# Two mixture-of-experts layers rewritten: one unrolled run of slots for all sequences, gate weights spread by one product, weights split two experts at a time

## The chip, the cores and the metric

The kernel runs on one core of one Trainium2 chip. The time is the device time of one launch in microseconds (us), the median of three runs. Engines are TensorE (PE; PEld is its weight load), VectorE (DVE), ScalarE (ACT), GpSimd (POOL) and SyncE (SP), which here only issues DMAs. Each engine runs its own instructions in order and waits on semaphores.

## What is computed

Ten layers in a row on eight sequences of 512 tokens with 128 features: rwkv, attn0, moe0, alibi, attn0, moe0, light, moe1, diff, moe1. The change touches only the four expert layers. Both kinds normalise the tokens, score eight experts, pick two and add the weighted sum of their outputs:

```
moe0: logits = xf @ Wr.T + expert_bias;  rw = softmax(logits);  topw, topi = top_k(rw, 2);  topw = softmax(topw)
      combine = sum(one_hot(topi, 8) * topw, axis=1)
      out = swiglu(xf, shared) + sum_e combine[:, e] * (silu(xf @ eW1[e]) * (xf @ eW3[e])) @ eW2[e]
moe1: the same without the bias and the shared expert, hidden size 256 (two tiles of 128) instead of 128
```

All experts are computed for all tokens; the weight of an expert that was not chosen is 0.

## The kernel before

**Slots.** A slot is one expert on one sequence. moe0 has 9 slots to a sequence (the shared expert first, then eight), with one tile (HT = 1); moe1 has 8 slots with two tiles (HT = 2). Every product of float32 data is three matmuls on rounded halves (`product`, lines 373 to 375): high by high, low by high, high by low. For each tile of a slot, TensorE makes `h1` and `h3` (3 matmuls each of 512 columns), ScalarE makes `s = silu(h1)` (L3267), `sc = s * bcs` scales it by the gate weight (POOL, L3301, or DVE, L3358), VectorE makes `g = sc * h3` (L3366), ScalarE rounds it to `g_hi` (L3239), VectorE makes `g_lo = g - g_hi` (L3337), and TensorE adds the `down` product (3 matmuls) into one PSUM bank, LAG = 2 slots later. `h1` and `h3` have two PSUM banks each.

**Gate weights.** `broadcast_c` makes the weight of expert e, one number a token, into a tile with the same row in all 128 partitions: four fp32 transposes (L3168) of a column of `comb` that is read as if it were 128 columns, then a ScalarE copy to `bcs` (L3251). The scaling is on DVE for all moe0 slots, and in moe1 on DVE for slot 1 and on POOL for the other seven.

**Head.** During the slots of sequence j, `Head` prepares sequence j+1: statistics (DVE, L203, L207), scale (POOL, L217 to L231), normalised tokens `z` (four DVE instructions, L256 or L258), four transposes, `hi` (ACT), `lo` (DVE), the gate product (12 matmuls of 8 columns), and on DVE `gate_logits`, `gate_choice`, `gate_weights`. moe0 also needs four small powers on POOL (`gate_exp`, L3109); both need one (`gate_e2`, L3114). The constants `E_STATS` to `E_WEIGHTS` say in which slot a part stands.

**Loop.** The slots stand in a hardware loop (`Fori`) over four pairs of sequences. A pass holds the slots of two sequences and ends by draining: the last two `down`, the output copy `out`, four transposes `tail` and the addition to `x`. The waits in the loop compare with registers that are worked out by extra instructions.

**Weights.** `Weights` loads the matrix in pieces of 1024 columns and splits each into high (ACT) and low (DVE) halves. All pieces are split before the loop; TensorE waits for all of them, and the gate choice of sequence 0 stands behind them on DVE.

Of the kernel before, what the change touches and what calls it, by code (L numbers as in the profile page):

```python
# [2962 lines left out]
def moe_block(core, name, moe, weights_in, kind, src, add_to, bias, store=False):  # L2963

# [10 lines left out]
    with ExitStack() as ctx:
        sb = lambda n, s, t=F32: ctx.enter_context(nc.sbuf_tensor(name + n, s, t))
        head = Head(core, ctx, name, kind, src, TR)
        vec, act = Steps(nc, ctx, plan, name + "_vector"), Steps(nc, ctx, plan, name + "_scalar")
# [46 lines left out]
        def gate_tensor(t, k, par):
            h = head
            t.wait_ge(h.act.sem, h.act.done(k, "hi"))
            t.wait_ge(h.low.sem, h.low.done(k, "lo"))
            t.wait_ge(h.vec.sem, h.vec.done(k, "logits", back=1))
            for q in range(NQ):  # L3030
                c = slice(q * P, (q + 1) * P)
                ins = product3(nc, ps[:, GATE, q * 8:q * 8 + 8], h.hi[:, par, c], h.lo[:, par, c], w_hi[:, 0:8], w_lo[:, 0:8])
            ins.then_inc(h.pe.sem, h.pe.step("gate"))


        def gate_logits(d, k):

            h, v, n = head, head.vec, nc.vector
            inc = lambda ins, *key: ins.then_inc(v.sem, v.step(*key))
            wait = lambda *key: d.wait_ge(v.sem, v.done(k, *key))  # L3040
            gate = ps[:, GATE, 0:NQ * 8].rearrange("p (q e) -> p q e", e=8)
            d.wait_ge(h.pe.sem, h.pe.done(k, "gate"))
            if bias is None:
                inc(n.tensor_copy(logits[:, :, :], gate), "logits")
            else:
                inc(n.tensor_tensor(logits[:, :, :], gate, bias_sb[:, :].unsqueeze(1).to_broadcast([P, NQ, 8]), ALU.add), "logits")
                wait("logits")
                inc(n.tensor_reduce(lmax[:, :], logits[:, :, :], AXX, ALU.max), "lmax")
                wait("lmax")
                inc(n.tensor_tensor(hot1[:, :, :], logits[:, :, :], wide(lmax[:, :]), ALU.subtract), "shifted")  # L3050
                wait("shifted")
                inc(n.tensor_scalar(hot2[:, :, :], hot1[:, :, :], LOG2E, None, ALU.mult), "shifted2")  # L3052

        def gate_choice(d, k):

            h, v, n = head, head.vec, nc.vector
            inc = lambda ins, *key: ins.then_inc(v.sem, v.step(*key))
            wait = lambda *key: d.wait_ge(v.sem, v.done(k, *key))
            if bias is None:
                wait("logits")  # L3060
            else:
                d.wait_ge(h.pool.sem, h.pool.done(k, "ex", NQ - 1))
                inc(n.reduce_sum(lsum[:, :], ex[:, :, :], AXX), "lsum")
                wait("lsum")
                inc(n.reciprocal(den[:, :], lsum[:, :]), "lrec")
                wait("lrec")
                inc(n.tensor_tensor(logits[:, :, :], ex[:, :, :], wide(den[:, :]), ALU.mult), "rw")
                wait("rw")
            settle(core, d)
            for q in range(NQ):  # L3070
                inc(n.max(top[:, q, :], logits[:, q, :]), "top", q)
            wait("top", NQ - 1)
            settle(core, d)
            inc(n.tensor_tensor(diff[:, :], top[:, :, 1], top[:, :, 0], ALU.subtract), "diff")
            for q in range(NQ):
                inc(n.max_index(idx[:, q, :], top[:, q, :], logits[:, q, :]), "idx", q)
            wait("diff")
            inc(n.tensor_scalar(p1[:, :], diff[:, :], LOG2E, None, ALU.mult), "diff2")
            wait("idx", NQ - 1)
            inc(n.tensor_copy(idxf[:, :, :], idx[:, :, 0:2]), "idxf")  # L3080
            wait("idxf")
            it = core.iota[:, :].unsqueeze(1).to_broadcast([P, NQ, 8])
            inc(n.tensor_tensor(hot1[:, :, :], idxf[:, :, 0:1].to_broadcast([P, NQ, 8]), it, ALU.is_equal), "hot1")
            inc(n.tensor_tensor(hot2[:, :, :], idxf[:, :, 1:2].to_broadcast([P, NQ, 8]), it, ALU.is_equal), "hot2")

        def gate_weights(d, k, par):

            h, v, n = head, head.vec, nc.vector
            inc = lambda ins, *key: ins.then_inc(v.sem, v.step(*key))
            wait = lambda *key: d.wait_ge(v.sem, v.done(k, *key))  # L3090
            d.wait_ge(h.pool.sem, h.pool.done(k, "e2"))
            inc(n.tensor_scalar(den[:, :], e2[:, :], 1.0, None, ALU.add), "den")
            wait("den")
            inc(n.reciprocal(p1[:, :], den[:, :]), "p1")
            wait("p1")
            inc(n.tensor_tensor(p2[:, :], p1[:, :], e2[:, :], ALU.mult), "p2")
            inc(n.tensor_tensor(hot1[:, :, :], hot1[:, :, :], wide(p1[:, :]), ALU.mult), "c1")
            wait("p2")
            inc(n.tensor_tensor(hot2[:, :, :], hot2[:, :, :], wide(p2[:, :]), ALU.mult), "c2")
            wait("c2")  # L3100
            inc(n.tensor_tensor(comb[:, par, :, :], hot1[:, :, :], hot2[:, :, :], ALU.add), "comb")

        def wide(a):
            return a.unsqueeze(2).to_broadcast([P, NQ, 8])

        def gate_exp(p, k, q):
            h, o = head, head.pool
            p.wait_ge(h.vec.sem, h.vec.done(k, "shifted2"))
            nc.gpsimd.tensor_tensor(ex[:, q, :], core.two[:, 0:8], hot2[:, q, :], ALU.pow).then_inc(o.sem, o.step("ex", q))  # L3109

        def gate_e2(p, k):
            h, o = head, head.pool
            p.wait_ge(h.vec.sem, h.vec.done(k, "diff2"))
            nc.gpsimd.tensor_tensor(e2[:, :], core.two[:, 0:NQ], p1[:, :], ALU.pow).then_inc(o.sem, o.step("e2"))  # L3114
# [4 lines left out]

        @block.sync
        def _(sp):
            if bias is not None:
                sp.dma_start(bias_sb[:, :], bias.unsqueeze(0).to_broadcast([P, 8])).then_inc(bias_loaded, 16)
            weights_in.sync_part(sp)
            if store:

# [1 line left out]
                with sp.Fori(0, PAIRS) as i:  # L3130
# [379 lines left out]
```

## Time and profile before

| what | value |
|---|---|
| median of three runs | 3336.51 us (3334.9 to 3336.55) |
| profiled execution | 3339.98 us, its span 3338.2 us |
| granted TensorE clock over the span | 0.909 of full |
| busy, share of span | PE 82%, DVE 65%, POOL 47%, ACT 44% |
| first moe0 layer | 532.7 to 821.2 us |
| second moe0 layer | 1158.5 to 1446.9 us |
| first moe1 layer | 1990.8 to 2379.5 us |
| second moe1 layer | 2950.5 to 3338.2 us |

Busy time is the time in which an engine works, a wait is the idle time ahead of an instruction with the one that released it. The layers follow each other with a barrier, so a layer's length adds directly to the whole. The four expert layers are 1353 us of 3338. Matmuls are pipelined, so that the distance from the start of one to the start of the next says what one costs, not its duration.

### The profile page before, as it was taken

What the parts mean: (1) busy time and instruction counts of PE and PEld (TensorE: products, weight loads), DVE (VectorE), ACT (ScalarE), POOL (GpSimd) and SP (SyncE); (2) the same over time, 40 slices, a digit from 0 to 9 for tenths busy, and PEclk for the clock granted to TensorE, in tenths of its full rate; (3) what the DMA queues carried; (4) which work ended last, traced back from release to release, by engine and by line L of the source; (5) the groups of instructions that cost most, each with busy time, mean ns of one, the idle gap of its engine ahead of it and who ended that gap; (6) DMA issues with size and microseconds to landing.
All of it is one profiled execution on the core that took longest, in us unless ns stands there. A gap on an engine that the chain in (4) does not pass through costs nothing. (4 is left out here: it accounts for less than half of the span.)

```text
span 3338.2 us, 51906 instructions
## 1 busy us (share of the span) xinstructions
PE 2741.1 (82%) x14536; PEld 1879.4 (56%) x14536; DVE 2169.6 (65%) x5031; ACT 1460.2 (44%) x2255; POOL 1576.9 (47%) x1513
## 2 busy tenths in 40 slices
PE   3367897887769878869889878899799999978898
PEld 2245565665656556645545446667555555556666
DVE  5745764776567477756555556666577777766666
ACT  3433454544425444521111114555366666645554
POOL 5544754333136433344444434444666666634444
PEclk7678798998779989979999999999799999989999
DMA  1000210000011100010000010000000000010000
GB/s 31 0 12 2 48 31 22 0 0 15 0 33 40 32 1 0 1 49 1 1 1 0 0 38 1 1 0 0 10 1 1 1 0 0 0 38 7 7 7 6
DMA packets 31343, 36.94 MB, mean 11 GB/s; under 512 B 11704, under 2 KB 20792, under 8 KB 30904
## 3 DMA queue, kind: packets, MB, share of 16 engines
q1 hardware_dynamic: 31160, 34.95, 3.7%
q8 instruction: 61, 1.00, 0.1%
q14 instruction: 122, 1.00, 0.1%
HBM read 20.11 MB, written 2.10 MB: 7 GB/s over the span
## 5 line engine op out<-in xcount | busy, mean ns | idle before, releaser
L1757 DVE TENSOR_REDUCE l_diffneg_max<-psum 128x1 fp32r<-128x512 f32 x536 | 363.9, 688 | 123.2 <-PE psum L1510 117.5
L3301 POOL TENSOR_TENSOR l_moe1sc<-l_moe1s,l_moe1bcs 128x512 f32<-128x512 f32 x224 | 300.6, 1350 | 283.9 <-ACT l_moe1s L3267 162.3
L1677 ACT ACTIVATE l_diffweights<-psum 128x1024 f32<-128x1024 f32 x256 | 262.2, 1025 | 155.7 <-PE psum L1537 153.7
L3366 DVE TENSOR_TENSOR l_moe1g<-l_moe1sc,psum 128x512 f32<-128x512 f32 x256 | 174.5, 681 | 217.3 <-POOL l_moe1sc L3301 180.2
L373 PE MATMUL psum<-l_moe1hi,l_moe1w_hi 128*128 128x512 f32 x512 | 222.4, 434 | 41.5 <-DVE l_moe1g L3366 28.8
L148 POOL TENSOR_TENSOR settled<-powers 128x1 f32<-128x1 f32 x133 | 38.4, 289 | 417.7 <-DVE l_moe0mv L207 115.7
L1510 PE MATMUL psum<-l_diffkz,l_diffQ 128*128 128x512 f32 x536 | 230.1, 430 | 0.3 <-DVE l_diffneg_max L1757 0.2
L3337 DVE TENSOR_TENSOR l_moe1g_lo<-l_moe1g,l_moe1g_hi 128x512 fp32r<-128x512 f32 x256 | 213.2, 835 | 0.0
L374 PE MATMUL psum<-l_moe1hi,l_moe1w_lo 128*128 128x512 f32 x512 | 204.6, 400 | 0.0
L375 PE MATMUL psum<-l_moe1lo,l_moe1w_hi 128*128 128x512 f32 x512 | 203.6, 398 | 0.0
L1088 DVE TENSOR_REDUCE l_attn0neg_max<-psum 128x1 fp32r<-128x512 f32 x256 | 167.1, 683 | 52.4 <-PE psum L831 49.7
L3109 POOL TENSOR_TENSOR l_moe0ex<-powers,l_moe0hot 128x8 f32<-128x8 f32 x72 | 118.4, 1670 | 164.8 <-DVE l_moe0hot L3052 164.8
L3267 ACT ACTIVATE l_moe1s<-psum 128x512 f32<-128x512 f32 x256 | 152.6, 597 | 94.4 <-PE psum L375 83.2
L1206 POOL TENSOR_TENSOR l_attn0half_sums<-l_attn0weights 128x2048 f32<-128x2048 f32 x30 | 137.2, 4574 | 105.1 <-ACT l_attn0weights L997 105.1
L2293 DVE TENSOR_TENSOR l_lightA<-psum,l_lightmask 128x512 f32<-128x512 f32 x130 | 83.7, 685 | 157.1 <-PE psum L2101 151.8
L997 ACT ACTIVATE l_attn0weights<-psum 128x1024 f32<-128x1024 f32 x128 | 130.1, 1022 | 111.1 <-PE psum L853 110.8
L3239 ACT ACTIVATE l_moe1g_hi<-l_moe1g 128x512 fp32r<-128x512 f32 x256 | 159.6, 624 | 31.0 <-DVE l_moe1g L3366 30.1
L1510 PEld LDWEIGHTS psum<-l_diffkz,l_diffQ 128*128 128x128 f32 x536 | 101.9, 190 | 123.1 <-issue 81.0
L1537 PE MATMUL psum<-l_diffQ,l_diffkz 128*128 128x512 f32 x512 | 162.5, 398 | 0.9 <-DVE l_diffneg_max L1757 0.9
L1890 POOL TENSOR_TENSOR l_difflow_rows<-l_diffwhole,l_diffmarks 128x512 fp32r<-128x512 f32 x70 | 72.8, 1039 | 191.2 <-ACT l_diffwhole L1661 185.5
L2204 ACT ACTIVATE l_lighto_hi<-psum 128x512 fp32r<-128x512 f32 x64 | 38.2, 597 | 257.7 <-PE psum L2134 175.0
L2393 POOL TENSOR_TENSOR x<-l_lightturned 128x512 f32<-128x512 f32 x68 | 87.1, 1280 | 129.3 <-DVE l_lightturned L2279 129.1
(466 smaller groups left out, 7894.5 us busy)
## 6 DMA issues: line engine op xcount, KB each, us to landing
l_attn0Q<-l_attn0q_hi SPq DMA_DIRECT2D x128, 64.0 KB, 2.0
l_moe1w_raw<-in_moe_w SPq DMA_DIRECT2D x12, 512.0 KB, 6.0
l_attn0Q<-l_attn0q_lo SPq DMA_DIRECT2D x64, 64.0 KB, 2.0
l_moe0w_raw<-in_moe_w SPq DMA_DIRECT2D x6, 512.0 KB, 4.7
x<-in_x SPq DMA_DIRECT2D x8, 256.0 KB, 4.6
out<-x SPq DMA_DIRECT2D x8, 256.0 KB, 2.3
x<-in_light_w SPq DMA_DIRECT2D x3, 512.0 KB, 4.6
l_attn0Q<-l_attn0max_rows SPq DMA_DIRECT2D x64, 2.0 KB, 1.7
```

The costliest lines, as they stand in the source:

```text
L373: nc.tensor.matmul(out, w_hi, x_hi, start=start, stop=False)
L374: nc.tensor.matmul(out, w_lo, x_hi, start=False, stop=False)
L375: return nc.tensor.matmul(out, w_hi, x_lo, start=False, stop=stop)
L1088: nc.vector.tensor_reduce(neg_max[:, n % 2, st, hh:hh + 1], ps[:, bank_of(("max", n, b)), :], AXX, ALU.max, negate=True).then_inc(vec_max. ...
L1510: nc.tensor.matmul(ps[:, bank, :], Q[:, n % 4, st * P:(st + 1) * P], kz[:, n % 4, hh, :], start=True, stop=True).then_inc(pe_max.sem, pe_m ...
L1537: ins = nc.tensor.matmul(ps[:, S[m % 2] + h, :], kz[:, n % 4, hh, tt * P:(tt + 1) * P], Q[:, n % 4, :], start=True, stop=True)
L1677: nc.scalar.activation(weights[:, tt, 2 * pair:2 * pair + 2, :], ps[:, S[m % 2]:S[m % 2] + 2, :], ACT.Exp, scale=SCALE).then_inc(act_exp.s ...
L1757: nc.vector.tensor_reduce(neg_max[:, n % 2, st, row:row + 1], ps[:, bank_of(("max", n, b)), :], AXX, ALU.max, negate=True).then_inc(vec_ma ...
L3239: nc.scalar.activation(g_hi[:, n % RING, h, :], g[:, n % 2, h, :], ACT.Copy).then_inc(act.sem, act.step("g_hi", u))
L3301: nc.gpsimd.tensor_tensor(sc[:, n % 2, h, :], s[:, n % 2, h, :], bcs[:, n % 2, :], ALU.mult).then_inc(pool.sem, pool.step("sc", u))
L3337: nc.vector.tensor_tensor(g_lo[:, n % RING, h, :], g[:, n % 2, h, :], g_hi[:, n % RING, h, :], ALU.subtract).then_inc(vec.sem, vec.step("g ...
L3366: nc.vector.tensor_tensor(g[:, n % 2, h, :], (s if is_shared(n) else sc)[:, n % 2, h, :], ps[:, H3[u % 2], :], ALU.mult).then_inc(vec.sem, ...
```

## The change

Only the expert layers change. What it does:

- The loop is unrolled: slots 0 to N-1 of all eight sequences (72 or 64) in one run, and there is one drain, at the end. Waits compare with constants.
- `comb`, now 128 x 4 x 40 with the weights in columns 0 to 7 and again in 32 to 39, is transposed once a sequence (`comb_turned`, 4 transposes), copied by ACT to high rows 0 to 39 (`comb_hi`) and turned into low rows 32 to 39 by DVE (`comb_lo`). A slot's weight is spread by one matmul of 512 columns (`weight_rows`, L3168): the stationary operand `pick` has ones in rows e and 32+e. ACT still copies the result to `bcs`.
- `h3` gets a third PSUM bank; all transposes and the gate share one bank (`MISC`). LAG is 3 in moe0.
- Scaling: moe0 slots 1, 2, 5 and 8 on POOL and 3, 4, 6 and 7 on DVE; moe1 as before.
- The tokens `z` are made by POOL with one (moe0) or two (moe1) 128x512 instructions instead of four on DVE, and statistics run two sequences ahead.
- `ExpertWeights` loads and splits the gate columns first, then two experts at a time (3 DMAs and 3 + 3 splits to a group); groups 0 and 1 before the run, the others in slots 0, 2 and 4 of sequence 0. On SyncE the bias of moe0 is issued behind the weights.

The core of the diff:

```
+    AT_ONCE = 2
+        for g in range(self.groups):
+            for span, _ in self.spans(g):
+                sp.dma_start(self.raw[:, span], self.core.dram[self.source][:, span]).then_inc(self.loaded[g], 16)
...
-    LAG, RING = 2, 4
-    H1, H3, BC, OUT, TR, GATE = (0, 1), (2, 3), 4, 5, 6, 7
+    LAG = 3 if moe.shared else 2
+    RING = 4
+    H1, H3, OUT, MISC, BC = (0, 1), (2, 3, 4), 5, 6, 7
+    N = NSEQ * NE
+    on_pool = lambda n: n % NE in ((1, 2, 5, 8) if moe.shared else (0, 2, 3, 4, 5, 6, 7))
+    AT_TR, AT_GATE, AT_LO, AT_LOGITS = 0, 2 if moe.shared else 1, 1 if moe.shared else 0, 2 if moe.shared else 1
+    AT_CHOICE, AT_E2, AT_WEIGHTS, AT_COMB = (5, 6, 7, 8) if moe.shared else (2, 2, 3, 5)
+    AT_STATS, AT_SCALE, AT_Z = (4, 6, 7) if moe.shared else (4, 4, 5)
...
-                for q in range(NQ):
-                    ins = nc.tensor.transpose(ps[:, BC, q * P:(q + 1) * P],
-                                              comb[:, j, q, e - moe.shared:e - moe.shared + 1].to_broadcast([P, P]),
-                                              core.ident[:, :])
+                nc.tensor.matmul(ps[:, BC, :], pick[:, e - moe.shared, :], comb_rows[:, j % 2, :], start=True, stop=True
+                                 ).then_inc(pe_bc.sem, pe_bc.step("row"))
...
+            for n in range(N + LAG + 1):
+                j, e = divmod(n, NE)
+                if n == 0 and moe.shared:
+                    up(0)
+                    comb_turned(0)
+                elif n == 0:
+                    comb_turned(0)
+                if real(n) and not is_shared(n):
+                    weight_rows(n)
+                if real(n) and not (n == 0 and moe.shared):
+                    up(n)
+                if real(n - LAG):
+                    down(n - LAG)
+                if e == LAG and 0 <= j - 1:
+                    tail(j - 1)
+                if e == AT_TR and j + 1 < NSEQ:
+                    head_turned(j + 1)
+                if e == AT_GATE and j + 1 < NSEQ:
+                    gate(j + 1)
+                if e == AT_COMB and j + 1 < NSEQ:
+                    comb_turned(j + 1)
...
+                if j + 2 < NSEQ:
+                    if e == AT_SCALE:
+                        token_scale(j + 2)
+                    if e == AT_Z:
+                        tokens(j + 2)
```

**TensorE, start of a moe0 layer.** `up(0)` and `up(1)` are the L373 to L375 rows on `l_moe0hi`, the L3168 rows the weight broadcasts of slots 1 and 2. Before:

```order
L373 MATMUL psum<-l_moe0hi,l_moe0w_hi 128x512
L374 MATMUL psum<-l_moe0hi,l_moe0w_lo 128x512
L375 MATMUL psum<-l_moe0lo,l_moe0w_hi 128x512
L3164 ISA
L3166 REGISTER_ALU
L3168 MATMUL psum<-ident,l_moe0comb 128x128 x4
L3166 ISA
L3168 MATMUL psum<-ident,l_moe0comb 128x128 x4
```

Now, from the first product of slot 0 to the broadcast of slot 2:

```order
L373 MATMUL psum<-l_moe0h_hi,l_moe0w_hi 128x512
L374 MATMUL psum<-l_moe0h_hi,l_moe0w_lo 128x512
L375 MATMUL psum<-l_moe0h_lo,l_moe0w_hi 128x512
L3213 MATMUL psum<-ident,l_moe0comb 40x128 x4
L3196 MATMUL psum<-ident,l_moe0z 128x128 x4
L3168 MATMUL psum<-l_moe0comb_rows,l_moe0pick 128x512
L373 MATMUL psum<-l_moe0h_hi,l_moe0w_hi 128x512
L374 MATMUL psum<-l_moe0h_hi,l_moe0w_lo 128x512
L375 MATMUL psum<-l_moe0h_lo,l_moe0w_hi 128x512
L3168 MATMUL psum<-l_moe0comb_rows,l_moe0pick 128x512
```

The products of slot 1 stood ahead of the first broadcast and now stand behind it; the turning of `comb` and the tokens of sequence 1 are new there.

**GpSimd, a moe1 layer in the middle of the run.** The L3301 rows (before) and L3547 rows (now) are the scalings, two to a slot. Before, from the statistics of the next sequence on:

```order
L148 TENSOR_TENSOR settled<-powers 128x1
L224 TENSOR_SCALAR l_moe1var<-l_moe1mv 128x4
L230 ISA
L231 TENSOR_TENSOR l_moe1scale<-l_moe1var,powers 128x4
L3298 REGISTER_ALU
L3300 ISA
L3301 TENSOR_TENSOR l_moe1sc<-l_moe1s,l_moe1bcs 128x512
```

Now:

```order
L3547 TENSOR_TENSOR l_moe1sc<-l_moe1s,l_moe1bcs 128x512 x8
L3538 TENSOR_TENSOR l_moe1e<-powers,l_moe1p 128x4
L3547 TENSOR_TENSOR l_moe1sc<-l_moe1s,l_moe1bcs 128x512 x4
L148 TENSOR_TENSOR settled<-powers 128x1
L3513 TENSOR_SCALAR l_moe1var<-l_moe1mv 128x4
L3515 TENSOR_TENSOR l_moe1scale<-l_moe1var,powers 128x4
L3547 TENSOR_TENSOR l_moe1sc<-l_moe1s,l_moe1bcs 128x512 x2
L3525 TENSOR_TENSOR l_moe1z<-x,l_moe1mv 128x512
L3527 TENSOR_TENSOR l_moe1z<-l_moe1z,l_moe1scale 128x512
```

The power of the gate stands between the scalings of slots 2 and 3, the scale of the tokens between slots 4 and 5, and the two token products, which are new on this queue, between slots 5 and 6. The scalings of slots 6, 7 and 0 of the next sequence are behind them.

## Rows read from the trace of the kernel before

**Rows 1.** The page's first line.
```profile
span 3338.2 us, 51906 instructions
```

**Rows 2.** Windows, the four expert stages: stretch, length, busy (instructions), PEclk, DMA.
```profile
532.70:821.20 288.50, 224.84 (x1080) 173.93 (x1080) 208.83 (x630) 138.69 (x234) 102.44 (x107) 0.90 0.02 6
...
1990.80:2379.50 388.70, 339.05 (x1584) 261.91 (x1584) 255.22 (x647) 197.85 (x344) 174.92 (x148) 0.96 0.02 9
2950.50:3338.20 387.70, 337.89 (x1584) 262.25 (x1584) 256.52 (x638) 203.11 (x348) 173.94 (x146) 0.96 0.04 13
```

**Rows 3.** Windows, one loop pass of the first and third stage.
```profile
562.35:629.14 66.79, 56.05 (x273) 43.00 (x272) 49.78 (x147) 34.74 (x59) 22.74 (x25) 0.94 0.00 1
2106.65:2197.70 91.05, 83.41 (x392) 64.22 (x392) 61.24 (x150) 47.47 (x84) 42.94 (x36) 0.98 0.00 0
```

**Rows 4.** Waits, first stage after its start: total us, times, longest.
```profile
POOL l_moe0ex L3109 <- DVE l_moe0hot L3052: 73.0, 8, 9.4
...
PE psum L373 <- DVE l_moe0g_lo L3337: 25.7, 20, 2.2
...
PE psum L3168 <- DVE l_moe0comb L3101: 12.5, 7, 2.1
```

**Rows 5.** Waits, third stage after its start.
```profile
DVE l_moe1g L3366 <- POOL l_moe1sc L3301: 92.0, 44, 5.0
...
PE psum L373 <- DVE l_moe1g L3366: 12.4, 21, 1.0
```

**Rows 6.** Timeline, TensorE around one weight broadcast, last stage: start, us.
```profile
3320.28 0.60 PE L3168 MATMUL psum<-ident,l_moe1comb 128*128 128x128 f32 x4
...
3320.64 0.48 PE L373 MATMUL psum<-l_moe1hi,l_moe1w_hi 128*128 128x512 f32 x1
...
3320.96 0.40 PE L374 MATMUL psum<-l_moe1hi,l_moe1w_lo 128*128 128x512 f32 x1
...
3321.19 0.39 PE L375 MATMUL psum<-l_moe1lo,l_moe1w_hi 128*128 128x512 f32 x1
```

**Rows 7.** Timeline, VectorE and GpSimd in one slot of the third stage.
```profile
2130.52 2.62 POOL L3301 TENSOR_TENSOR l_moe1sc<-l_moe1s,l_moe1bcs 128x512 f32<-128x512 f32 x2 [3.33 <-ACT l_moe1s L3267]
...
2132.03 0.69 DVE L3366 TENSOR_TENSOR l_moe1g<-l_moe1sc,psum 128x512 f32<-128x512 f32 x1 [2.99 <-POOL l_moe1sc L3301]
...
2132.63 1.05 DVE L3337 TENSOR_TENSOR l_moe1g_lo<-l_moe1g,l_moe1g_hi 128x512 fp32r<-128x512 f32 x1
...
2134.21 0.68 DVE L3337 TENSOR_TENSOR l_moe1g_lo<-l_moe1g,l_moe1g_hi 128x512 fp32r<-128x512 f32 x1
```

**Rows 8.** Timeline, start of the first stage.
```profile
546.64 7.57 POOL L3109 TENSOR_TENSOR l_moe0ex<-powers,l_moe0hot 128x8 f32<-128x8 f32 x4 [8.98 <-DVE l_moe0hot L3052]
...
558.12 0.19 DVE L3101 TENSOR_TENSOR l_moe0comb<-l_moe0hot 128x32 f32<-128x32 f32 x1
```

**Rows 9.** Timeline, start of the third stage.
```profile
2002.89 5.83 DVE L360 TENSOR_TENSOR l_moe1w_lo<-l_moe1w_raw,l_moe1w_hi 128x1024 fp32r<-128x1024 f32 x6
...
2014.93 0.60 ACT L3251 ACTIVATE l_moe1bcs<-psum 128x512 f32<-128x512 f32 x1 [0.94 <-PE psum L3168]
```

**Rows 10.** Timeline, GpSimd in one sequence of the first stage.
```profile
639.57 6.46 POOL L3109 TENSOR_TENSOR l_moe0ex<-powers,l_moe0hot 128x8 f32<-128x8 f32 x4 [9.15 <-DVE l_moe0hot L3052]
652.00 1.01 POOL L3114 TENSOR_TENSOR l_moe0e<-powers,l_moe0p 128x4 f32<-128x4 f32 x1 [5.98 <-DVE l_moe0p L3078]
```

**Rows 11.** Groups of GpSimd, the nearest to the new token products: busy us, mean ns.
```profile
L1188 POOL TENSOR_TENSOR l_attn0z<-x,l_attn0scale 128x512 f32<-128x512 f32 x16 | 16.8, 1049 | 3.9 <-PE psum L798 1.9
...
L244 POOL TENSOR_TENSOR l_rwkvtkeep<-x,l_rwkvtmv 128x512 f32<-128x512 f32 x10 | 13.1, 1310 | 2.0 <-POOL l_rwkvtrstd L239 1.9
```

**Rows 12.** Groups of VectorE that share ports or move.
```profile
L3337 DVE TENSOR_TENSOR l_moe1g_lo<-l_moe1g,l_moe1g_hi 128x512 fp32r<-128x512 f32 x256 | 213.2, 835 | 0.0
...
L256 DVE TENSOR_SCALAR l_moe0z<-x,l_moe0scale 128x128 f32 (+1 forms) x72 | 30.4, 482 | 19.9 <-POOL l_moe0scale L231 19.7
```

**Rows 13.** Timeline, weight loads queued on SyncE, first stage.
```profile
534.54 1.85 SPq L326 DMA_DIRECT2D l_moe0w_raw<-in_moe_w  x4
```

More of the change, by code:

```diff
@@ L3025, in gate_tensor @@
[L3025 to L3029, printed above, removed]
-            for q in range(NQ):
[L3031 to L3044, printed above, removed]
-            else:
[L3046 to L3114, printed above, removed]
@@ new lines, in moe_block, with misc_free, scaled @@
+        misc = [("tr", 0), ("gate", 0), ("comb", 0)] + [u for n in range(N + LAG + 1) for u in misc_users(n)]
+        before = {u: misc[k - 1] for k, u in enumerate(misc) if k}
+        def misc_free(t, user):
+            if user in before:
+                what, j = before[user]
+                of, step = {"tail": (vec_tail, "tail"), "tr": (vec_lo, "lo"), "gate": (vec_gate, "logits"), "comb": (vec_comb, "lo")}[what]
+                t.wait_ge(of.sem, of.done(j, step))
+        def scaled(n, h):
+            of = pool_sc if on_pool(n) else vec_sc
+            return of.sem, of.done(scaled_before(n), "sc", h)
@@ L3198, in tail @@
[L3198 to L3224 removed]
+                ins.then_inc(pe_down.sem, pe_down.step("down"))
@@ new lines, in _, with head_hi, comb_hi @@
+            for of in (act_silu, act_ghi, act_bc, act_out, act_hi, act_comb):
+                of.credit(a)
+            copy = lambda to, frm: nc.scalar.activation(to, frm, ACT.Copy)
+            def head_hi(j):
+                act_hi.start()
+                a.wait_ge(pe_tr.sem, pe_tr.done(j, "tr"))
+                copy(h_hi[:, j % 2, :], ps[:, MISC, :]).then_inc(act_hi.sem, act_hi.step("hi"))
+            def comb_hi(j):
+                act_comb.start()
+                a.wait_ge(pe_comb.sem, pe_comb.done(j, "comb"))
+                copy(comb_rows[:, j % 2, :], ps[0:ROWS, MISC, :]).then_inc(act_comb.sem, act_comb.step("hi"))
@@ new lines, in add @@
+            def add(j):
+                pool_added.start()
+                at = slice(j * T, (j + 1) * T)
+                nc.gpsimd.tensor_tensor(add_to[:, at], add_to[:, at], src[:, at], ALU.add).then_inc(pool_added.sem, pool_added.step("added"))
+            token_scale(0)
+            tokens(0)
+            p.memset(comb[:, :, :], 0.0).then_inc(comb_cleared, 1)
+            if bias is not None:
+                for q in range(NQ):
+                    gate_exp(0, q)
+            gate_e2(0)
```

694 lines of the change are left out of this document (443 added, 251 removed).

## The prediction

> **What bounds the kernel now.** I read four views in this order. The windows by layer give the stakes: the expert layers take 288.5, 288.4, 388.7 and 387.7 us of the span of 3338.2 [rows 1, 2]. The two of a kind are alike, so I work on the first moe0 and the first moe1 layer. No engine is full in them: in moe0 TensorE is busy 225 of 288.5 us and DVE 209, in moe1 TensorE 339 of 388.7 [rows 2]. One pass of the loop, two sequences, takes 66.8 us in moe0 and 91.05 in moe1 [rows 3].
>
> What must TensorE do in a pass? In a dense place matmuls of 512 columns start 0.23 us apart, the four fp32 transposes of a broadcast hold it for 0.36, and the first matmul behind them needs 0.32 instead of 0.23 [rows 6]. So a broadcast costs 0.45. A moe1 slot is 18 x 0.233 + 0.45 = 4.64 us, a sequence 37.1, and with the next sequence's head (four transposes 0.45, twelve gate matmuls about 1.35) and tail (0.45) 39.4, or 79 a pass: TensorE is held up for about 12 of 91 us. For moe0, 81 x 0.233 + 8 x 0.45 + 2.25 = 24.7 a sequence, 49.5 a pass: 17 of 67 us are lost.
>
> The waits name the holders. In moe0 TensorE waits for `g_lo` (25.7 us in all, up to 2.2 at once: the drains at the end of a pass, and DVE behind its gate work) and for `comb` (12.5) [rows 4]. In moe1 DVE waits 92.0 us for POOL's scaling and TensorE then 12.4 for `g`, which frees an `h3` bank [rows 5]. The chain of a slot is seen in moe1: POOL's two scalings take 2.62, `g` starts at 1.5 us after the first begins, `g_lo` follows [rows 7].
>
> **The change part by part.** *Broadcast.* One matmul, 0.233, for 0.45, and 0.45 once a sequence for turning `comb`. TensorE's own work becomes 8 x 4.42 + 2.7 = 38.05 us a moe1 sequence and 81 x 0.233 + 8 x 0.233 + 2.7 = 23.4 a moe0 sequence. DVE and ACT get one 0.6 to 0.7 us instruction each a sequence (`comb_lo`, `comb_hi`). That the 40-row matmul costs as much as a 128-row one is my choice; with the cost of the transposes it replaces it would be 0.45, 1.8 us more a sequence.
>
> *Drain.* Three of four drains vanish; the next sequence's slots run across.
>
> *Load.* `z` leaves DVE (four instructions of 0.48 in moe0 [rows 12]) and goes to POOL. The nearest POOL rows for a 128x512 product with a spread operand are 1.05 and 1.31 [rows 11]; I take 1.3, the slower, for the layers' other 128x512 work on POOL costs that. That is 1.3 in moe0, 2.6 in moe1. In moe0 four of eight scalings leave DVE. Its sequence then holds 9 `g` and 9 `g_lo` at 0.60 apart (the step from `g` to `g_lo` in [rows 7]), 4 scalings at 0.9, `lo`, `comb_lo` and tail 1.8, statistics 1.4, gate 4.2: 21.8 us, below TensorE's 23.4. POOL holds 4 x 1.3 + 6.5 + 1.0 [rows 10] + scale 1.9 + tokens 1.3 + addition 1.3 = 17.2. In moe1 DVE has 30 and POOL 24 of 38. So TensorE is the longest everywhere, and what is left is order. I walk one sequence in the middle of the run, us from the start of a slot, with the durations above, ACT 0.6.
>
> *moe0.* Slot 1 starts at 0. The gate at the end of slot 2 (4.66) waits for `lo`, behind slot 1's DVE work: 5.3, **0.65 lost**. Logits end at 7.75, POOL's four powers at 14.25 (6.46 [rows 10]), so the scaling of slot 5 runs 14.3 to 15.6, `g` to 16.4, choice 17.0 to 19.2. DVE then brings `g_lo` of slot 5 at 21.4, where `down(5)` in slot 8 would start at 20.4: **1.1 lost**. The gate's weights are behind slot 7 on DVE and end at 24.75; TensorE stands at the turning of `comb` from 22.2: **2.6 lost**. What is queued behind that turning is all of the next sequence. Slot 8's scaling on POOL, behind the power, the scale and the tokens, is 3 us late (22.9), and the slack of LAG 3 hides it. Period 23.4 + 4.35 = 27.75, now 33.4.
>
> *moe1.* Slot 0 at 0. POOL waits in slot 2 for the gate's difference, made at the end of DVE's slot 2 (18.5), and the scalings of slot 3 are 2.1 late. It waits again for the statistics (28.7), so slot 5's scalings start at 30.4, 4.1 late. With the tokens between, slot 6's start at 35.4. The third `h3` bank and the two slots of lag hide all but: `h3` of slot 6's second tile waits for `g` of slot 5 (**1.1**), `down(4)` second tile (**0.75**), `down(5)` second tile (**0.5**). With 0.1 in slot 4, period 38.05 + 2.45 = 40.5, now 45.5.
>
> *Start and end.* moe0: the powers of sequence 0 start about 1.2 us earlier than at 546.64, since only three small splits lie ahead, and `comb` is ready at 556.8 instead of 558.1 [rows 8]. But turning, `comb_hi`, and on DVE a weight group (1.1), statistics (1.4), `g` of slot 0 and `comb_lo` follow, so slot 1 starts at 560.6, 27.9 us into the layer, on a TensorE that has idled. On SyncE the bias is now behind 17 issues of 0.46 [rows 13]: it is issued at 541.5 and must still land, and the logits need it at 544.3. I add 0.5. Layer: 27.9 + 8 x 27.75 + 0.5 = 250.4 against 288.0 without the gap after it: **-37.6**. The last sequence has no head and no stalls (-7), the drain gives that back.
>
> moe1: the 5.83 us of low halves [rows 9] shrink to 2.0 ahead of the choice, tokens cost 1.5 more on POOL, and turning, copy, second group, statistics and `comb_lo` add 4. Slot 0 begins at 2012.5, where `bcs` was copied at 2014.9 [rows 9] with slot 0's products already done. Layer: 21.8 + 8 x 40.5 + 2.5 of drain = 348.3 against 388.4: **-40.1**. Splitting the later groups inside sequence 0 (1.8 us of DVE each) and the cold clock are covered by slots 0 and 1 having no `down`; if not, 2 us a layer.
>
> Sum: 2 x 37.6 + 2 x 40.1 = 155 us off the span. The profiled execution took 3339.98, the median 3336.5, 0.1% less, so I subtract from the median: **3181 us**.
>
> **A rule against it.** DVE's `g_lo` took 1.05 us beside a POOL scaling and 0.68 where POOL was idle [rows 7]; over moe1 its mean is 835 ns [rows 12]. The moe0 layer gets POOL scalings, so its two-input DVE work meets the same. The Trainium skill, SBUF — State Buffer, Who interferes with whom, says that a DVE instruction with two SBUF inputs and a GpSimd instruction that reads SBUF exclude each other for a whole instruction. The 1.05 agrees: that `g_lo` ended 0.54 after POOL did.
>
> **The rivals.** *Port.* POOL's wide work covers 7.9 of 27.75 us in a moe0 sequence; 13 DVE instructions, each meeting it with that chance for half of 1.3 us, give 2.4 us. If this lies fully on TensorE's path it costs 2.4 x 16 = 38: **3219**. For it: [rows 12]. Against: DVE has 5 us to spare. *Slack is larger than walked.* All stalls vanish (DVE waits end earlier, the banks hide them): 4.35 and 2.45 less for 7 sequences of two layers each, 95 us: **3086**. Against: in-order waits of 2 to 4 us are the rule in [rows 4]. *In-order POOL passes everything on (the slower side).* Place: POOL's queue, where the scale, power and tokens wait for DVE and the scalings stand behind. If each lateness reached TensorE whole, moe1 would have 38.05 + 2.1 + 4.1 + 3.1, about 47.3 a sequence (403 the layer, +14.5) and moe0, where 0.7 and 3 add to the 4.35, 31.5 (280, -8): twice the difference is +13 us, **3350**. The layers break even at 32.4 and 45.5 us a sequence. Against: today POOL is idle for long and DVE catches up in a slot. *The change does nothing*: only if the four layers are held by something not in these rows; I see none.
>
> **How the numbers follow.** Likeliest 3181, 0.58, its own range 3150 to 3205 (1 us a sequence either way over 32 sequences). Port or similar extra waits 0.20, slack larger 0.15 (seldom in full), slower 0.04, nothing 0.03. The range 3095 to 3235 leaves out some 0.15. A difference of 0.2% is about what this measurement can tell from none: faster 0.93, same 0.03, slower 0.04.
>
> **What would show it.** The windows of the layers: near 250 and 348 us. L3168 rows with single 512-column matmuls 0.23 before the next. In moe0 TensorE's largest wait a sequence is for `comb`, about 2.6 us, then `g_lo`; in moe1 for `g` and `g_lo` late in the sequence, released behind POOL. Slot 1 of moe0 starts near 28 us, slot 0 of moe1 near 22. The other six layers keep their lengths. I am wrong if moe0 is above 33 us a sequence, if the 40-row product costs 0.45, or if the unrolled code shows waits that no engine releases.

## The result

The changed kernel takes **3325.18 us** (median of 7 runs, 3313.18 to 3329.75), the kernel before in runs beside it 3336.55 (7 runs, 3334.9 to 3348.92). The ratio is **0.995, interval 0.9928 to 0.9971**: faster by half a per cent, 11 us, where I had forecast 155.

The span of the profiled execution is 3327.4 us, with 45520 instructions for 51906. These are the windows of the four expert layers (stretch, length, busy of PE, PEld, DVE, ACT, POOL with instructions, granted clock, DMA). A layer is taken here from the last write of `x` ahead of it to its own last write of `x`, and the last layer to the end of the span.

```profile
537.70:833.05 295.35, 240.51 (x904) 167.10 (x904) 192.45 (x554) 139.40 (x249) 140.57 (x129) 0.86 0.02 7
1175.42:1471.10 295.68, 241.20 (x904) 167.83 (x904) 192.26 (x554) 139.26 (x249) 141.31 (x129) 0.86 0.02 7
2001.28:2377.42 376.14, 345.62 (x1408) 247.78 (x1408) 262.65 (x598) 202.96 (x357) 193.81 (x161) 0.96 0.03 9
2948.54:3327.40 378.86, 343.50 (x1408) 246.05 (x1408) 263.35 (x598) 203.94 (x358) 194.09 (x161) 0.96 0.05 15
```

Against [rows 2] the reader is to see three things. The moe1 layers got 12 us shorter. The moe0 layers got **longer**, by 7 and 6 us. And TensorE is busier in moe0 (240.5 us for 224.8) although it has 904 records where it had 1080, at a lower clock, 0.86 for 0.90. By the same bounds, this is where all kernels of this study spend their span. The lengths are from the one profiled execution of each kernel, the median is of all its runs; the last column is what lies outside the expert layers:

| kernel | median us | ratio to before, interval | moe0 | moe0 | moe1 | moe1 | rest |
|---|---|---|---|---|---|---|---|
| before | 3336.55 | | 288.0 | 289.8 | 387.9 | 391.1 | 1981.4 |
| changed | 3325.18 | 0.995, 0.9928 to 0.9971 | 295.3 | 295.7 | 376.1 | 378.9 | 1981.4 |
| rows64 | 3316.46 | 0.9928, 0.9908 to 0.9948 | 292.1 | 292.9 | 375.8 | 378.4 | 1970.2 |
| pool_early | 3302.79 | 0.9884, 0.9867 to 0.99 | 288.5 | 284.9 | 376.2 | 379.2 | 1973.7 |
| filled | 3284.77 | 0.9836, 0.9817 to 0.9854 | 281.4 | 280.7 | 376.7 | 378.9 | 1965.5 |
| rows128 | 3282.9 | 0.9833, 0.9814 to 0.9852 | 285.9 | 286.4 | 364.3 | 367.7 | 1977.0 |
| turned_back | 3247.33 | 0.9716, 0.9699 to 0.9732 | 266.7 | 271.5 | 367.8 | 373.0 | 1969.6 |
| order1 | 3238.1 | 0.9688, 0.967 to 0.9706 | 285.7 | 287.3 | 343.5 | 348.4 | 1971.9 |
| early0 | 3228.64 | 0.9665, 0.9638 to 0.9693 | 261.5 | 259.6 | 365.1 | 369.6 | 1973.9 |
| both | 3191.21 | 0.9562, 0.9534 to 0.959 | 262.0 | 257.4 | 343.5 | 347.5 | 1970.7 |
| both_turned | 3151.81 | 0.9429, 0.9413 to 0.9444 | 246.0 | 246.8 | 345.3 | 348.5 | 1973.1 |

One `rows64` run (4410.02 us at a granted clock of 0.549) and one run of before (3470.34 us at 0.787) are slow runs and are left out of the ratios. The rest moves by up to 16 us with no edit in it, so an effect is read from the layers, and the whole only confirms it. (The median of before was 3341.99, 3342.64 and 3338.82 beside the three groups of experiments, so the ratios are the better column.)

**A sequence.** Windows of sequence 3 of the first moe0 layer and of the first moe1 layer, from the first silu of one sequence to that of the next:

```profile
670.30:704.10 33.80, 29.62 (x114) 20.59 (x114) 23.58 (x67) 16.55 (x29) 17.61 (x16) 0.90 0.00 1
2159.57:2203.66 44.09, 42.45 (x178) 30.40 (x177) 31.97 (x74) 24.61 (x44) 24.41 (x20) 1.00 0.00 1
```

The six sequences from 1 to 6 of moe0 take 32.4 to 33.8 us, 33.1 in the mean, where half a pass of [rows 3] is 33.4; those of moe1 take 44.1 (only the sixth, with no statistics left to make, 41.6) for 45.5. I had forecast 27.75 and 40.5. Yet the waits are as small as forecast. TensorE's waits in these stretches (total us, times, longest), moe0 and then moe1, against [rows 4] and [rows 5]:

```profile
PE psum L3213 <- DVE l_moe0comb L3405: 23.4, 6, 4.0
...
PE psum L373 <- DVE l_moe1g_lo L3437: 8.0, 15, 0.7
PE psum L373 <- DVE l_moe1g L3430: 3.2, 6, 0.5
```

In moe0 one wait of 3.9 us is left in a sequence, for `comb`; in moe1 some 1.6. So it is TensorE's own work (the time of a sequence less these waits) that is too long. Here is a weight spread inside one slot of moe0, TensorE's matmuls and then its weight loads (start, us, instruction), to be read against [rows 6]:

```profile
674.72 0.40 PE L375 MATMUL psum<-l_moe0g_lo,l_moe0w_hi 128*128 128x512 f32 x1
675.05 0.49 PE L3168 MATMUL psum<-l_moe0comb_rows,l_moe0pick 40*128 40x512 f32 x1
675.47 0.49 PE L373 MATMUL psum<-l_moe0h_hi,l_moe0w_hi 128*128 128x512 f32 x1
675.80 0.40 PE L374 MATMUL psum<-l_moe0h_hi,l_moe0w_lo 128*128 128x512 f32 x1
```

```profile
674.49 0.19 PEld L375 LDWEIGHTS psum<-l_moe0g_lo,l_moe0w_hi 128*128 128x128 f32 x1
675.05 0.18 PEld L3168 LDWEIGHTS psum<-l_moe0comb_rows,l_moe0pick 40*128 40x128 f32 x1 [0.37 <-issue]
675.47 0.19 PEld L373 LDWEIGHTS psum<-l_moe0h_hi,l_moe0w_hi 128*128 128x128 f32 x1 [0.24 <-issue]
```

The steps are 0.33, 0.42 and 0.33 where dense ones are 0.23: the one product costs 1.08 less two dense steps, **0.62 us**, not 0.233, and more than the 0.455 of the four transposes it replaced. The loads say why. The load for L375 starts with the matmul ahead of it, 0.23 before its own; that for the 40-row product starts only with its own matmul, and so does the full one behind it. No matmul waits for another engine in this stretch, so the waits of PE don't show it.

The second cause is the low clock. TensorE behind the wait for `comb`:

```profile
701.71 1.01 PE L3213 MATMUL psum<-ident,l_moe0comb 128*40 128x128 f32 x4 [4.04 <-DVE l_moe0comb L3405]
702.38 0.78 PE L373 MATMUL psum<-l_moe0h_hi,l_moe0w_hi 128*128 128x512 f32 x1
702.95 0.63 PE L374 MATMUL psum<-l_moe0h_hi,l_moe0w_lo 128*128 128x512 f32 x1
703.38 0.63 PE L375 MATMUL psum<-l_moe0h_lo,l_moe0w_hi 128*128 128x512 f32 x1
...
705.05 0.39 PE L373 MATMUL psum<-l_moe0g_hi,l_moe0w_hi 128*128 128x512 f32 x1
```

The steps are 0.43 until shortly before 705.05, and the granted clock from 702.00 to 705.00 is 0.50, the lower level of 1.2 GHz. A second such stretch comes in slot 3: 0.51 from 681.2 to 684.6. And here is what lengthened that wait, VectorE and GpSimd just ahead of it:

```profile
697.49 1.24 POOL L3523 TENSOR_TENSOR l_moe0z<-x,l_moe0scale 128x512 f32<-128x512 f32 x1
697.75 1.00 DVE L3392 TENSOR_SCALAR l_moe0den<-l_moe0e 128x4 f32<-128x4 f32 x1
698.69 1.26 POOL L3547 TENSOR_TENSOR l_moe0sc<-l_moe0s,l_moe0bcs 128x512 f32<-128x512 f32 x1
...
699.00 0.97 DVE L3396 TENSOR_TENSOR l_moe0p<-l_moe0p,l_moe0e 128x4 f32<-128x4 f32 x1
...
699.91 1.28 POOL L3553 TENSOR_TENSOR x<-x 128x512 f32<-128x512 f32 x1
700.00 1.24 DVE L3399 TENSOR_TENSOR l_moe0hot<-l_moe0hot,l_moe0p 128x32 f32<-128x32 f32 x1
```

Three DVE instructions on 4 or 32 elements, 0.16 to 0.19 us each where GpSimd is idle, took 1.00, 0.97 and 1.24: each ended within 0.1 us of a wide GpSimd instruction. In moe1 it is `g_lo` that got longer, in the mean 936 ns for 835 in [rows 12]:

```profile
L3437 DVE TENSOR_TENSOR l_moe1g_lo<-l_moe1g,l_moe1g_hi 128x512 fp32r<-128x512 f32 x256 | 239.3, 936 | 0.0
```

### The profile page after: what moved, and what is told of

Its sections match the earlier page's. It is cut to its first block and busy times, and to the rows that moved or that the text cites. A ratio compares the mean times of both kernels' runs of the same rounds, so it can differ in the third digit from the quotient of the medians.

```text
span 3327.4 us, 45520 instructions
## 1 busy us (share of the span) xinstructions
PE 2785.1 (84%) x13832; PEld 1834.1 (55%) x13832; DVE 2147.6 (65%) x4781; ACT 1467.9 (44%) x2308; POOL 1693.1 (51%) x1583
## 5 line engine op out<-in xcount | busy, mean ns | idle before, releaser
L1757 DVE TENSOR_REDUCE l_diffneg_max<-psum 128x1 fp32r<-128x512 f32 x536 | 364.3, 688 | 124.9 <-PE psum L1510 119.5
L3547 POOL TENSOR_TENSOR l_moe1sc<-l_moe1s,l_moe1bcs 128x512 f32<-128x512 f32 x224 | 306.0, 1378 | 207.8 <-ACT l_moe1s L3271 201.1
L3437 DVE TENSOR_TENSOR l_moe1g_lo<-l_moe1g,l_moe1g_hi 128x512 fp32r<-128x512 f32 x256 | 239.3, 936 | 0.0
L373 PE MATMUL psum<-l_moe1h_hi,l_moe1w_hi 128*128 128x512 f32 x512 | 219.9, 430 | 7.0 <-DVE l_moe1g L3430 7.0
L148 POOL TENSOR_TENSOR settled<-powers 128x1 f32<-128x1 f32 x111 | 30.8, 277 | 365.4 <-DVE l_alibimv L207 106.3
L374 PE MATMUL psum<-l_moe1h_hi,l_moe1w_lo 128*128 128x512 f32 x512 | 205.3, 401 | 0.0
L375 PE MATMUL psum<-l_moe1h_lo,l_moe1w_hi 128*128 128x512 f32 x512 | 204.4, 399 | 0.0
L3547 POOL TENSOR_TENSOR l_moe0sc<-l_moe0s,l_moe0bcs 128x512 f32<-128x512 f32 x64 | 82.1, 1283 | 182.2 <-ACT l_moe0s L3271 148.6
L3430 DVE TENSOR_TENSOR l_moe0g<-l_moe0sc,psum 128x512 f32<-128x512 f32 x128 | 87.9, 687 | 106.6 <-POOL l_moe0sc L3547 92.3
```

What stands on the lines that cost most here:

```text
L373: nc.tensor.matmul(out, w_hi, x_hi, start=start, stop=False)
L374: nc.tensor.matmul(out, w_lo, x_hi, start=False, stop=False)
L375: return nc.tensor.matmul(out, w_hi, x_lo, start=False, stop=stop)
L1757: nc.vector.tensor_reduce(neg_max[:, n % 2, st, row:row + 1], ps[:, bank_of(("max", n, b)), :], AXX, ALU.max, negate=True).then_inc(vec_ma ...
L3430: v.tensor_tensor(g[:, n % 2, h, :], (s if is_shared(n) else sc)[:, n % 2, h, :], ps[:, H3[(n * HT + h) % 3], :], ALU.mult).then_inc(vec_g ...
L3437: v.tensor_tensor(g_lo[:, n % RING, h, :], g[:, n % 2, h, :], g_hi[:, n % RING, h, :], ALU.subtract).then_inc(vec_glo.sem, vec_glo.step("l ...
```

## The experiments

Theory A: the 40-row product costs TensorE 0.62. B, its rival: any single product does, or its time is hidden. C: GpSimd's wide work stretches the gate chain. D (moe1) and E (moe0): what then waits is the order of small steps on POOL and DVE. F: the idle stretch itself brings the low clock. The other parts of the change (the unrolled loop, the third bank, LAG, the split of the scalings, the loading of the weights) were not taken apart.

**Full rows.** The same product over 128 rows, the added ones zero (and 64 rows in the other kernel):

```
-    ROWS = LO_ROW + 8
+    ROWS = P          # rows64: 64
```

> The changed kernel with 128 rows instead of 40 in comb, comb_rows and pick (rows 40 to 127 zero, same result). Theory A (a product that uses only part of the 128 rows does not overlap with the full-row products before and behind it, so it costs 0.62 us of TensorE and not 0.233): the step from L375 to L3168 falls from 0.327 to 0.23, from L3168 to L373 from 0.424 to 0.23, from L373 to L374 behind it from 0.335 to 0.23; a moe1 sequence falls from 44.1 to 41.0 us, a moe0 sequence from 33.2 to 30.1, the whole by 32 x 3.1 = 99 us to 3226. Rival B (every single product with a stationary operand of its own costs this, or its time is hidden under waits): the steps stay and the time stays within 10 us of 3325.

> The same with 64 rows. If only a product over all 128 rows overlaps with its neighbours (theory A), the steps stay at 0.33, 0.42 and 0.33 and the time at 3325. If it is the odd 40 that costs, it falls like the kernel with 128 rows, to 3226.

Ratio 0.9833 for rows128, 3282.9 us; 0.9928 for rows64, level with the changed kernel (0.995) within the intervals. One spread with 64 rows, then one with 128, moe1:

```profile
2145.96 0.40 PE L375 MATMUL psum<-l_moe1g_lo,l_moe1w_hi 128*128 128x512 f32 x1
2146.29 0.50 PE L3168 MATMUL psum<-l_moe1comb_rows,l_moe1pick 64*128 64x512 f32 x1
2146.72 0.50 PE L373 MATMUL psum<-l_moe1h_hi,l_moe1w_hi 128*128 128x512 f32 x1
2147.06 0.39 PE L374 MATMUL psum<-l_moe1h_hi,l_moe1w_lo 128*128 128x512 f32 x1
```

```profile
2151.46 0.40 PE L375 MATMUL psum<-l_moe1g_lo,l_moe1w_hi 128*128 128x512 f32 x1
2151.69 0.40 PE L3168 MATMUL psum<-l_moe1comb_rows,l_moe1pick 128*128 128x512 f32 x1
2151.92 0.39 PE L373 MATMUL psum<-l_moe1h_hi,l_moe1w_hi 128*128 128x512 f32 x1
```

With 128 rows the steps are 0.23, with 64 they stay at 0.33, 0.43 and 0.34. Theory A holds for 40 and 64 rows, step by step, and B falls: 88 more rows, of zeros, make the product 0.39 us cheaper. The Trainium skill, TensorE: Matmul & The Clock Gate, LDWEIGHTS, says that a load of 32 rows takes as long as one of 128; the loads' durations agree (0.18 us for 40 or 64 rows, 0.19 for 128). What differs is when they start: that of the 128-row product at 2151.46, 0.23 ahead of its matmul, that of the 64-row one at 2146.28, 0.01 ahead.

Theory A says "only part of the 128 rows", and that is too wide. In the attn0 layers of the kernel before, 97-row products stand behind 128-row ones:

```profile
448.15 0.39 PE L375 MATMUL psum<-l_attn0h_lo,l_attn0w_hi 128*128 128x512 f32 x1
448.38 0.64 PE L853 MATMUL psum<-l_attn0Q,l_attn0K 97*128 97x512 f32 x2
```

The first of them starts 0.23 to 0.24 behind its neighbour in all 20 such places, and the second 0.23 to 0.24 behind the first. So the overlap is lost somewhere between 64 and 97 rows; where, and why, no run here shows.

The size was a miss, 42 us for 99. A moe1 sequence fell by 1.1 only, mostly because TensorE's waits in it rose from 1.6 to 3.1 us. A moe0 sequence fell by 0.5, because its waits rose from 3.9 to 5.6 (that for `comb` to 4.8) and its granted clock fell from 0.91 to 0.89. Under the slow product lay a second limit at nearly the same height.

**The old broadcast in the new kernel.** Four transposes a slot again, no turning of `comb`:

```
+                for q in range(NQ):
+                    ins = nc.tensor.transpose(ps[:, BC, q * P:(q + 1) * P],
+                                              comb[:, j % 2, q, e - moe.shared:e - moe.shared + 1].to_broadcast([P, P]), core.ident[:, :])
-                nc.tensor.matmul(ps[:, BC, :], pick[:, e - moe.shared, :], comb_rows[:, j % 2, :], start=True, stop=True
```

> The changed kernel with the broadcast of the kernel before (four fp32 transposes of a comb column for each slot, no turning of comb, no comb_rows), all else as changed. Theory A: a slot's broadcast costs 0.45 instead of 0.62 and the turning (0.55 a sequence) goes: 1.9 us a sequence; in moe0 comb is first needed a slot later, 2.8 us less of the wait for it in 14 turns: 32 x 1.9 + 14 x 2.8 = 100, total 3225. If the product were as cheap as predicted (0.233), going back would cost 32 x 8 x 0.22 = 56 us less 14 x 2.8, total 3325 + 17 = 3342.

0.9716, 3247.33 us, forecast 3225: undoing this one part takes 78 us off. The layers fall by 29, 24, 8 and 6 us, 67 in all; the remainder lies in the unchanged layers. The spread by a product, as written, cost time in all four. In moe0 a part of this is that `comb` is needed a slot later: the wait for it is 1.9 us for 3.9.

**GpSimd's wide work moved off the gate weights (moe0).**

```
-    AT_STATS, AT_SCALE, AT_Z = (4, 6, 7) ...
+    AT_STATS, AT_SCALE, AT_Z = (3, 5, 5) ...
-                if e == 0 and add_to is not None:
+                if e == 2 and add_to is not None:
```

> The changed kernel with POOL's statistics-to-tokens work of moe0 moved so that it does not lie beside DVE's gate weights: statistics in slot 3, scale and tokens in slot 5, addition in slot 2. Theory C (DVE's small instructions of 0.17 to 0.19 us took 1.00, 0.97 and 1.24 beside POOL's wide ones, and TensorE's wait of 4.4 us for comb holds these 2.7 us): they fall to 0.2 or at most one stays long, the wait for comb falls to 1.7 to 2.7, a moe0 sequence by 2 to 2.7 us, the total by 14 x 2.3 = 32 to 3293. Rival (DVE arrives at the gate weights late anyway, or the work moved now delays the powers): no change within 5 us, or slower.

0.9884, 3302.79 us, forecast 3293. The groups of the three instructions, six sequences: the changed kernel, then this one.

```profile
L3392 DVE TENSOR_SCALAR l_moe0den<-l_moe0e 128x4 f32<-128x4 f32 x6 | 6.5, 1078 | 0.0
L3399 DVE TENSOR_TENSOR l_moe0hot<-l_moe0hot,l_moe0p 128x32 f32<-128x32 f32 x6 | 5.3, 888 | 0.0
L3396 DVE TENSOR_TENSOR l_moe0p<-l_moe0p,l_moe0e 128x4 f32<-128x4 f32 x6 | 5.0, 833 | 0.2
```

```profile
L3399 DVE TENSOR_TENSOR l_moe0hot<-l_moe0hot,l_moe0p 128x32 f32<-128x32 f32 x6 | 1.2, 192 | 0.0
...
L3396 DVE TENSOR_TENSOR l_moe0p<-l_moe0p,l_moe0e 128x4 f32<-128x4 f32 x6 | 1.0, 162 | 0.2
L3392 DVE TENSOR_SCALAR l_moe0den<-l_moe0e 128x4 f32<-128x4 f32 x6 | 0.9, 156 | 0.0
```

2.8 us became 0.5. The wait for `comb` fell from 3.9 to 2.8 us only, a sequence from 33.1 to 31.5 at a clock of 0.93 for 0.91, the moe0 layers by 7 and 11. Theory C holds, at two thirds of the size for the whole.

**Idle time filled.** Sixteen products that nobody needs, in front of the wait for `comb` (moe0):

```
+                if j >= 1 and moe.shared:
+                    for _ in range(16):
+                        nc.tensor.matmul(ps[:, MISC, :], w_hi[:, moe.w1:moe.w1 + P], h_hi[:, j % 2, :], start=True, stop=True)
```

> The changed kernel with 16 products of 512 columns added in moe0 ahead of each wait for comb (into the free MISC bank, overwritten by the turning): work that the result doesn't need, 16 x 0.233 = 3.7 us a sequence in the place of the idle 4.4. Theory F (TensorE runs at half clock behind that wait because it stood idle, 1.3 to 3.5 us a sequence): the granted clock of a sequence rises from 0.91 to 0.96 or more, a sequence gets 1 to 2.5 us shorter although work is added, the total by 14 x 1.7 = 24 to 3301. Rival (the low clock has nothing to do with the wait): the clock stays at 0.91, no gain (3325), or the 16 products take 6.8 us at half clock and the time goes up by 14 x 2.4 = 34 to 3359.

0.9836, 3284.77 us, forecast 3301: 224 matmuls more, and 40 us less, of which 29 are in the two moe0 layers (14 and 15) and the other layers' drift is the remainder. One place and one window of 31 us:

```profile
691.74 3.88 PE L3213 MATMUL psum<-l_moe0h_hi,l_moe0w_hi 128*128 128x512 f32 x16
695.93 0.61 PE L3216 MATMUL psum<-ident,l_moe0comb 128*40 128x128 f32 x4 [0.31 <-DVE l_moe0comb L3408]
696.30 0.48 PE L373 MATMUL psum<-l_moe0h_hi,l_moe0w_hi 128*128 128x512 f32 x1
```

```profile
636.00:667.00 31.00, 30.54 (x131) 21.82 (x130) 23.61 (x68) 16.62 (x31) 17.68 (x16) 1.00 0.00 1
```

Behind the turning (its four transposes, then the first matmul in 0.37) there are no 0.43 steps. In ten of the twelve sequences in the middle of the two layers the granted clock is 1.00 for 0.90 to 0.92, and such a sequence takes 30.9 us for 33.1 (the other two are at 0.95). Theory F holds for this wait. The second slow stretch of a sequence went too in these ten, though nothing was added there.

**Order of the small steps.** In moe1 on top of rows128, in moe0 on top of it, and both:

```
order1   AT_CHOICE, AT_E2, AT_WEIGHTS, AT_COMB = 2, 3, 4, 5 (was 2, 2, 3, 5); AT_STATS, AT_SCALE, AT_Z = 4, 5, 6 (was 4, 4, 5)
early0   AT_CHOICE, AT_E2, AT_WEIGHTS, AT_COMB = 4, 5, 5, 7 (was 5, 6, 7, 8); AT_STATS, AT_SCALE, AT_Z = 3, 5, 5; addition in slot 2
```

> The kernel with 128 rows (3282.9), and in moe1 three small POOL steps behind the scalings that they held up: the power of the gate behind slot 3 instead of 2, the scale behind slot 5 instead of 4, the tokens behind slot 6 instead of 5; gate weights on DVE in slot 4. Theory D (the 3.1 us that TensorE still waits in a moe1 sequence come from POOL waiting 3.5 us for the gate's difference and 4.8 us for the statistics with scalings behind): the waits fall to 0.5 or less, a sequence from 43.0 to 40.3, the total by 16 x 2.7 = 43 to 3240. Rival (the two token products on POOL and DVE's g_lo of 1.1 us beside them are the cause): the waits stay at 2 to 3 us, the total within 15 us of 3283.

> The kernel with 128 rows (3282.9), and in moe0 the chain from the powers to comb a slot or two earlier: choice in slot 4, power and weights in slot 5, turning of comb behind slot 7, and statistics in slot 3, scale and tokens in slot 5, addition in slot 2. Theory E (the wait of 4.8 us for comb is a matter of order alone, and the half clock behind it is its consequence): the wait falls to 0.3 or less, the granted clock of a sequence rises from 0.85 or 0.93 to 0.97 or more, a moe0 sequence falls from 32.6 to 26.3, the total by 14 x 6.3 = 88 to 3195. If the clock stays low for another reason (the gate's small products), only the wait goes: 14 x 4.8 = 67, total 3216. If the powers on POOL really set the pace, a new wait for g_lo behind the choice takes its place and the total stays above 3250.

> 128 rows with both new orders. If the layers are independent, the two gains add: 3283 - 43 - 88 = 3152.

> Both new orders with the four transposes a slot of the kernel before and no turning. By the steps measured (0.455 against 0.233 a slot, less 0.45 for the turning) it is 8 x 0.22 - 0.45 = 1.3 us a sequence slower than the one with 128 rows: 3152 + 32 x 1.3 = 3194, less some 3 us a layer at the start, where the turning, copy and low half are not waited for: 3182. If waits other than these set the time, the two are equal.

order1: 3238.1 us, forecast 3240. TensorE's and GpSimd's waits in moe1 behind its start, rows128 and then order1:

```profile
PE psum L373 <- DVE l_moe1g_lo L3437: 10.8, 17, 0.7
PE psum L373 <- DVE l_moe1g L3430: 5.9, 5, 1.2
...
POOL settled L148 <- DVE l_moe1mv L3331: 23.8, 5, 4.8
POOL l_moe1e L3538 <- DVE l_moe1p L3381: 21.3, 6, 3.5
```

```profile
PE psum L3213 <- DVE l_moe1comb L3405: 4.4, 6, 0.7
...
POOL l_moe1sc L3547 <- ACT l_moe1s L3271: 106.5, 43, 7.9
```

GpSimd now waits for nothing but the silu, nothing stands behind a statistic or a gate step, and a sequence takes 39.4 us for 43.0. Theory D holds. Its rival (the token products on GpSimd, and `g_lo` made longer by them) falls: both are still there, `g_lo` with 940 ns in the mean for 934.

early0: 3228.64, off by 34 us from the forecast and by 13 from its other branch. The wait for `comb` fell to 0.2, but one of 2.0 us came for `h_lo` ahead of the gate, and the clock stayed at 0.89 to 0.94 in most sequences. So theory E holds for the wait and not for the clock, which is low here with no wait above 2.0 us. both: 3191.21 (3182.99 to 3205.51), forecast 3152 from early0's optimistic forecast; from the gains measured (45 and 54) it is 3184. Its layers are those of early0 and of order1 within 2.2 us each, so layer by layer the gains add.

both_turned: **3151.81**, 30 us under the forecast and the fastest. Its moe0 sequences take 26.6 us at a granted clock of 1.00, the wait for `h_lo` is 0.3 for 2.0, and the waits of a sequence are 1.1 in all for 2.8. By the steps alone it should have been slower than both. It is the port again. The DVE instruction ahead of `h_lo`, with GpSimd's scaling beside it, in both and then in both_turned:

```profile
655.21 1.27 POOL L3547 TENSOR_TENSOR l_moe0sc<-l_moe0s,l_moe0bcs 128x512 f32<-128x512 f32 x1 [0.49 <-issue]
655.41 1.62 DVE L3437 TENSOR_TENSOR l_moe0g_lo<-l_moe0g,l_moe0g_hi 128x512 fp32r<-128x512 f32 x1
```

```profile
655.66 0.68 DVE L3423 TENSOR_TENSOR l_moe0g_lo<-l_moe0g,l_moe0g_hi 128x512 fp32r<-128x512 f32 x1
656.23 1.27 POOL L3526 TENSOR_TENSOR l_moe0sc<-l_moe0s,l_moe0bcs 128x512 f32<-128x512 f32 x1 [1.26 <-ACT l_moe0bcs L3239]
```

In both the scaling starts 0.2 ahead of `g_lo`, which then takes 1.62; in both_turned `bcs` comes later, the scaling starts 0.57 behind it, and it takes 0.68. That is 0.94 of the 1.7 us. TensorE also gets to the gate later behind its slower spreads: 0.4, counted from the tokens' transposes. The low half of `comb` is not the cause: turned_back has none, and it has the wait of 2.0 and a `g_lo` of 1.69. In the one sequence of the twelve of both where that `g_lo` takes 0.69, the wait is 0.5. No run moves this scaling alone, so the cause is read from the traces and not tested; by them the gain hangs on where two instructions happen to lie. The four layers take 246.0, 246.8, 345.3 and 348.5 us, the lengths that I had forecast for the change (250 and 348).

## Why the prediction was wrong

Two of its own signs of being wrong came: a moe0 sequence above 33 us (33.1), and a 40-row product at least as dear as the transposes it replaces (0.62 for 0.455).

**The sum.** By its own steps, a sequence in us; "own" is the period less TensorE's waits, in sequence 3.

| | own, forecast | own, measured | waits, forecast | waits, measured | period |
|---|---|---|---|---|---|
| moe0 | 23.4 | 29.8 | 4.35 | 4.0 | 27.75, measured 33.8 (mean 33.1) |
| moe1 | 38.05 | 42.5 | 2.45 | 1.6 | 40.5, measured 44.1 |

**The step that failed first** is "That the 40-row matmul costs as much as a 128-row one is my choice; with the cost of the transposes it replaces it would be 0.45". It is 0.62: 0.39 more in 8 slots is 3.1 us a sequence, 99 of the 144 us in question. Even my upper bound was too low, since I bounded an operation of a new shape by the one that it replaces. rows128 takes the excess away and rows64 doesn't, so the cost of the product is shown; that it was worth 42 us at once and the rest only with what waited beneath it mended, too. In order1, with full rows and 0.7 us of waits, a moe1 sequence has 38.7 us of own work, near the 38.05 of the sum.

**The second** is the clock, which the sum took as full. In `filled` the filling and the wait behind it take the same 4.0 us as the wait alone did, and a sequence takes 30.9 us at full clock. So of the 33.8 us of sequence 3 some 2.9 are the clock, and 2.2 of the mean 33.1. [rows 3] had 0.94 in a moe0 pass, and I used the pitch of a dense place of moe1.

**The third** is the size of the wait for `comb`, 3.9 for 2.6. The two other stalls that I had walked in moe0 (0.65, 1.1) did not appear: the total of the waits came out right by two errors. The rival *Port* had the mechanism and nearly the price (2.4 us a sequence; the three instructions are 2.3 longer in the mean), but not the place: in the changed kernel it is not the wide `g_lo` that matters, it is the chain of tiny instructions. And not all of it lay on TensorE's path: pool_early took the 2.3 us away, and the wait for `comb` fell by 1.1.

**Point by point.** Drain: gone, as said. Start of moe1: slot 0 at 2023.4, 22.1 us into the layer, forecast 21.8. Start of moe0: slot 1 at 569.1, 31.4 us in, forecast 27.9. `comb` was on time (24.4 us into the layer, at 562.1; forecast 24.1), and the low half of `comb` was done on DVE at 565.8, 28.1 us in. But TensorE then stood for the tokens of sequence 1:

```profile
568.09 1.09 PE L3196 MATMUL psum<-ident,l_moe0z 128*128 128x128 f32 x4 [4.75 <-POOL l_moe0z L3523]
569.11 0.79 PE L3168 MATMUL psum<-l_moe0comb_rows,l_moe0pick 40*128 40x512 f32 x1
```

They stand ahead of the first spread on TensorE, as the order of instructions shown with the change had it; I had left them out: 3.3 of the 3.5 us. The first sequence after that runs at a granted clock of 0.74 and takes 35.2 us to the first silu of the next. The sum had no term for this in moe0; for moe1 it had "covered by slots 0 and 1 having no `down`", which nearly held (45.6 and 44.3 us for 44.1). GpSimd's in-order rival was real (order1: 45 us of the whole), but beneath the slow product it was hidden. In moe1 TensorE waits for `g` and `g_lo`, as forecast. The other six layers keep their sum, 1981.4 us both times, not their lengths: both attn0 layers are 6 us longer and the light layer 14 shorter.

**Where the gain went:** 16 sequences of moe1 gain 1.4 us each, and moe0 gains 0.3, while its start, first sequence and end together lose 9 us a layer. What was forecast was there, but paid for with a product that did not overlap, and in moe0 with the clock. What stays open: why the second slow stretch of a moe0 sequence comes where it does, and why early0 keeps a low clock with no wait above 2.0 us. In moe1 both_turned is 0.2 us a sequence slower than both, where its steps say 1.3: the wait of 0.7 for `comb` went with the turning, and 0.4 stays open.
